# Third layer of a four-layer kernel: passage and tile order rebuilt, routing spread over the tiles, and the experts begun where the tile loop ends

## The reference

```python
proj = x @ W_in.T + b_in                      # gate, h (32 heads of 64), B, C (128 each), dt (32)
hBC = silu(conv(hBC, conv_w))                 # causal, 4 taps
dt = softplus(dt + dt_bias)
Adt = A * dt
A_cum = cumsum(A_c)                           # in chunks
Y_diag = einsum(C_c B_c * exp(segsum(A_c)), h_c)
states, carried from chunk to chunk with exp(sum of Adt)
Y_off = einsum(C_c, states) * exp(A_cum)
y = Y_diag + Y_off + D * h
g = y * silu(gate)
g = g * rsqrt(mean(g * g, -1) + EPS) * norm_w
return g @ W_out.T + b_out
```

## Time and profile before

| | |
|---|---|
| median of 3 runs | 1264.71 us (1264.55 to 1265.39) |
| profiled execution | 1266.14 us |
| its span, first to last instruction | 1264.4 us |
| busy in the span: PE, DVE, ACT, POOL | 1134.3, 899.1, 794.3, 564.4 us |
| chain that ended last, shares of the span | PE 43%, DVE 29%, ACT 15%, issue 7%, POOL 5% |

### The profile page before, as it was taken

One profiled execution on the slowest core, in us unless ns is written; L12 is line 12 of the kernel. 1 busy time (PEld: TensorE's weight loads), 2 busy tenths in 40 slices (PEclk: granted clock), 3 DMA queues, 4 the chain that ended last, 5 costly groups with the idle time before them and its releaser, 6 DMA issues.

```text
span 1264.4 us, 14530 instructions
## 1 busy us (share of the span) xinstructions
PE 1134.3 (90%) x4940; PEld 611.8 (48%) x4940; DVE 899.1 (71%) x1361; ACT 794.3 (63%) x1118; POOL 564.4 (45%) x308
## 2 busy tenths in 40 slices
PE   6788999999989999999768999999999999897887
PEld 1333344444334444444446666666666666222554
DVE  3666999999974545434589989899899998323454
ACT  4467667667542433323578888888988887435542
POOL 6002899898933846431004545545455455200000
PEclk8879999999999999999789999999999999798999
DMA  3000655555442211110021212112111111000000
GB/s 124 1 1 19 221 183 176 196 177 188 171 160 59 60 42 42 36 45 1 1 72 30 59 52 59 52 44 59 52 55 55 44 59 37 1 0 1 1 1 34
DMA packets 36807, 84.22 MB, mean 67 GB/s; under 512 B 7253, under 2 KB 13174, under 8 KB 36470
## 3 DMA queue, kind: packets, MB, share of 16 engines
q1 hardware_dynamic: 36734, 83.29, 20.9%
HBM read 80.72 MB, written 2.56 MB: 66 GB/s over the span
## 4 chain that ended last, share of the span: by engine, by line
PE 43%; DVE 29%; ACT 15%; issue 7%; POOL 5%; DMA 1%; DVEq 0%; SPq 0%; POOLq 0%; ACTq 0%
DVE work L1572 7%; DVE work L660 6%; PE ps L1010 4%; PE ps L1267 4%; PE ps L1234 4%; PE ps L1026 3%; PE ps L1018 3%; DVE yd L1633 3%; ACT work L1430 3%; ACT work L1425 3%; ACT ps L557 3%; POOL work L721 2%; DVE work L1636 2%; PE ps L441 2%; PE ps L1841 2%
## 5 line engine op out<-in xcount | busy, mean ns | idle before, releaser
L1706 POOL TENSOR_TENSOR ssum<-ssum,rs 128x1024 f32<-128x1024 f32 x32 | 75.8, 2369 | 192.9 <-DVE work L1572 190.6
L660 DVE TENSOR_TENSOR_SCAN work<-ps,work 128x1024 f32<-128x1024 f32 x64 | 146.6, 2291 | 8.3
L1572 DVE SCALAR_TENSOR_TENSOR work<-work,w_t 128x1024 f32<-128x1024 f32 x96 | 123.3, 1285 | 33.6 <-ACT work L1430 31.3
L441 PE MATMUL ps<-work,ident 128*128 128x512 f32 x256 | 121.7, 598 | 5.6 <-POOL work L721 5.4
L1000 POOL TENSOR_TENSOR work<-work,ssum 128x1024 f32<-128x1024 f32 x32 | 76.3, 2389 | 108.9 <-DVE work L1089 56.4
L557 ACT ACTIVATE ps<-work,A 128x1024 f32<-128x1024 f32 x64 | 71.6, 1118 | 72.4 <-DVE work L660 72.4
L1089 DVE TENSOR_TENSOR work<-work,ps 128x512 f32<-128x512 f32 x64 | 43.8, 687 | 99.9 <-PE ps L1018 99.8
L1068 ACT ACTIVATE work<-ps 128x512 f32<-128x512 f32 x64 | 38.1, 597 | 115.4 <-PE ps L1010 115.3
L721 POOL TENSOR_TENSOR work<-work 128x1024 f32<-128x1024 f32 x42 | 99.1, 2362 | 13.5 <-DVE work L660 13.5
L1714 POOL TENSOR_TENSOR yd<-yd,work 128x896 f32<-128x896 f32 x32 | 67.0, 2094 | 70.2 <-DVE work L1636 70.2
L1623 DVE SCALAR_TENSOR_TENSOR work<-ps,work 128x512 f32<-128x512 f32 x128 | 81.9, 682 | 0.0
(11 more groups left out here) (349 smaller groups left out, 2546.6 us busy)
## 6 DMA issues: line engine op xcount, KB each, us to landing
work<-bc_rows SPq DMA_DIRECT2D x42, 512.0 KB, 3.5
work<-sdo_rows SPq DMA_DIRECT2D x64, 224.0 KB, 3.6
yd<-bc_rows SPq DMA_DIRECT2D x22, 512.0 KB, 3.7
rs<-w_rows SPq DMA_DIRECT2D x32, 256.0 KB, 4.1
ssum<-share_rows SPq DMA_DIRECT2D x32, 256.0 KB, 3.2
w_t<-in_tile_w SPq DMA_DIRECT2D x32, 195.5 KB, 2.5
work<-in_w SPq DMA_DIRECT2D x1, 2048.0 KB, 7.9
shared<-in_f SPq DMA_DIRECT2D x3, 512.0 KB, 5.9
```

Of the source, the lines that this page charges most:

```text
L441: mm = pe.matmul(ps[:, YACC + h, :], ident[:, :], HS[u % 4][:, h * BL:(h + 1) * BL], start=(n == 0), stop=(n == DS - 1))
L660: dve.tensor_tensor_scan(h, flat_pair(DABANK), h, 0.0, ALU.mult, ALU.add).then_inc(m0["scan"], 1)
L1572: c = dve.scalar_tensor_tensor(HC[u], HP[:, tap:tap + SEQ], par(u, "taps", tap), HC[u], ALU.mult, ALU.add)
```

## The change

- Passage: B and C of the first sequence alone are prepared ahead of the loop. Step sizes and logits are one matmul of 40 columns, the logits' sigmoid is Exp on ScalarE and a sum and reciprocal on VectorE. `later`, a third triangular matrix, gives the decays in one matmul.
- The second sequence's B and C, and all routing, are done in the tiles: `beside(n)` at the head of VectorE's step, turned B in tile `B1_TURN` = 10, products in tile 11, routing in tiles 17 to 24, turned in tiles 25 and 26. In those four tiles TensorE uses `FRONT` first, and the projection of the next h comes behind the products with the states and a wait for the copy out of `FRONT`.
- Tile order: `ystar` goes ahead of the convolution; Silu of h is two halves; both halves of h are turned ahead of the first arguments.
- End: `f2_pe` starts behind the last tile's products. The last output sum and the mean squares lie between the experts; Ln and Exp are two instructions of 2048 behind the last Gelu, and VectorE scales after the last weighing.

```diff
@@ l2_sync
-                sp.wait_ge(m2["hc"], n + 1)
+                sp.wait_ge(m2["hc"], 2 * n + 2)
...
+                if n == 2:
+                    store_rows(1)
+                    store_decays(1)
@@ l2_pe, step
+                if n in (B1_TURN, B1_PRODUCT, ROUTE_TURN, ROUTE_TURN + 1):
+                    if n >= ROUTE_TURN:
+                        turn_route(n - ROUTE_TURN)
+                    else:
+                        second_sequence(n)
+                    from_states(n, b, 0)
+                    from_states(n, b, 1)
+                    if n >= ROUTE_TURN:
+                        pe.wait_ge(f2["rt_out"], n - ROUTE_TURN + 1)
+                    elif n == B1_TURN:
+                        pe.wait_ge(m2["act"], m2["bt_out1"] + 2)
+                    else:
+                        pe.wait_ge(m2["dve"], m2["gt_out1"] + 2)
                     project_h(m, b1, u1)
+                    within_chunks(n)
                     project_gate(m, b1, u1)
+                else:
...
                     turn_h(m, u1, 0)
+                    turn_h(m, u1, 1)
                     pe.wait_ge(m2["yd"], n + 1)
                     arguments(m, u1, (0, 1))
-                    turn_h(m, u1, 1)
@@ l2_act, step
+                if n == 1:
+                    decay_rows(2)
+                    decay_rows(3)
+                if n == B1_TURN:
+                    b_turned(1)
                 if more:
                     pad_h(n + 1, 1 - u)
                 if n >= 1:
                     squares(n - 1, 1 - u)
                 if more:
-                    silus(n + 1, 1 - u)
+                    silu_gate(n + 1, 1 - u)
+                    silu_h(n + 1, 1 - u)
+                    if n == B1_TURN - 1:
+                        bc_silu(1, 0)
+                        bc_silu(1, 1)
                     exponentials(n + 1)
                     weights_out(n + 1, 1 - u)
+                if n in (B1_CONV - 1, B1_CONV):
+                    bc_first_tap(1, n - B1_CONV + 1)
+                if n == ROUTE_TURN + 2:
+                    act.wait_ge(f2["rt_out"], 2)
+                    act.activation(rtb[:, :], rtf[:, :], ACT.Copy).then_inc(f2["rt_out"], 1)
@@ l2_dve
+            def beside(n):
+                if n < 2:
+                    if n == 1:
+                        dve.wait_ge(m2["dve"], m2["parts1"] + 1)
+                    three_parts(2 + n, LNDT[0:2 * H2, :, :].rearrange("p i h -> p (i h)"))
+                elif B1_CONV <= n < B1_CONV + 2 * K3:
+                    m, i = divmod(n - B1_CONV, K3)
+                    dve.wait_ge(m2["bc_tap"], 3 + m)
...
+                elif n == B1_PRODUCT:
+                    mask_products(1)
...
@@ l2_dve, step
+                beside(n)
+                dve.wait_ge((m2["sdo_in0"], m2["sdo_in1"])[u], 32 * (n // 2 + 1))
+                dve.wait_ge(m2["yoff"], 2 * n + 2)
+                dve.tensor_tensor(Y[u][:, P:], Y[u][:, P:], flat2(MID)[:, P:], ALU.mult).then_inc(m2["ystar"], 1)
                 if m < CT * BATCH:
                     convolve(m, 1 - u)
@@ f2_act
+                if n == NB * per:
+                    act.wait_ge(m2["act"], m2["rms_out"] + NB)
+                    act.preload_act_table_set("natural_log_exp_and_others")
+                    own(act.activation(flat(0, T), flat(0, T), ACT.Ln, bias=eps_t[:, :]))
+                    act.activation(flat(0, T), flat(0, T), ACT.Exp, scale=-0.5).then_inc(m2["act"], NB)
@@ f2_dve
+            scale_sums(dve, own)
             gate_dve(dve, own, f2, m2["dve"], m2["s_out"])
```

More of the change, by code:

```diff
@@ L290, in norm_act @@
             for k in range(NB):
+                if between is not None and k == NB - 1:
+                    between(0)
                 act.wait_ge(norm["centred"], NB * r + k + 1)
@@ L297, in norm_act, with top2_part @@
             root(NB - 1)
[L299 removed]
+        def top2_part(dve, own, score, ind, k, half):
             cur, eq, t, pick = rw[:, 2], rw[:, 3], rw[:, 4], rw[:, 5]
             bc = lambda m: m.unsqueeze(2).to_broadcast([P, NT, E])
[L303 to L304 removed]
+            s = score if k == 0 else cur
+            if half == 0:
                 own(dve.tensor_reduce(rm[:, 0, :], s, AX.X, ALU.max))
@@ L314, in top2 @@
                     own(dve.tensor_tensor(ind, ind, pick, ALU.add))
+        def top2(dve, own, score, ind):
+            for part in range(4):
+                top2_part(dve, own, score, ind, *divmod(part, 2))
         def split3(dve, own, w):
@@ L1294, in sum_out, with turn_route, second_sequence @@
                 mm.then_inc(m2["outp"], 1)
+            def turn_route(half):
+                pe.wait_ge(f2["dve"], f2["picked"] + 1)
+                for i in range(TB):
+                    mm = pe.transpose(ps[0:4 * E, FRONT + i // 4, (i % 4) * P:(i % 4 + 1) * P], rt[:, half * TB + i, :], ident[:, :])
+                mm.then_inc(f2["pe"], 1)
+            def second_sequence(n):
+                pe.wait_ge(m2["act"], m2["bc1"] + 2)
+                for c in range(TB):
+                    if n == B1_TURN:
+                        mm = pe.transpose(four(FRONT + c // 4)[:, c % 4, :], tile(BCH[0], TB + c), ident[:, :])
+                    else:
+                        mm = pe.matmul(four(FRONT + c // 4)[:, c % 4, :], tile(BCH[0], TB + c), tile(BCH[1], TB + c), start=True, stop=True)
+                    if c % 4 == 3:
+                        mm.then_inc(m2["pe"], 1)
             def step(n, b, t, u):
@@ new lines, in while_normed, with sums_turned @@
+            def while_normed(k):
+                if k == 0:
+                    project_bc(0, BACK)
+                if k == 1:
+                    steps_and_logits(0)
+                    steps_and_logits(1)
+                if k == 2:
+                    pe.wait_ge(m2["bc_pad"], 2)
+                    project_bc(1, BACK)
+                if k >= 2:
+                    steps_and_logits(k)
+            def sums_turned(k):
+                for i in range(8 * k, 8 * k + 8):
+                    here = slice((i % 4) * P, (i % 4 + 1) * P)
+                    pe.matmul(ps[0:H2, 4 + i // 4, here], ADT[:, i, :], upper[:, :], start=True, stop=True)
+                    pe.matmul(ps[H2:2 * H2, 4 + i // 4, here], LNDT[:, i, :], ident[:, :], start=True, stop=False)
+                    mm = pe.matmul(ps[H2:2 * H2, 4 + i // 4, here], ADT[:, i, :], fall[:, :], start=False, stop=True)
+                mm.then_inc(m2["pe"], 1)
@@ L1365, in l2_pe @@
                 mm.then_inc(m2["pe"], 1)
-            for k in range(NB):
-                if k == 2:
-                    turn_h(0, 0, 0)
-                    turn_h(0, 0, 1)
-                    pe.wait_ge(m2["act"], m2["bt_out"] + NB)
-                for i in range(4):
-                    c = 4 * k + i
-                    mm = pe.matmul(four(GT_BANK[k])[:, i, :], tile(BCH[0], c), tile(BCH[1], c), start=True, stop=True)
-                mm.then_inc(m2["pe"], 1)
-            pe.wait_ge(m2["rows_const"], 1)
+            pe.wait_ge(m2["bc_pad"], 8)
@@ L1377, in l2_pe @@
+            sums_turned(1)
+            pe.wait_ge(m2["act"], m2["cdec"] + 1)
+            for c in range(TB):
+                mm = pe.matmul(four(MID + c // 4)[:, c % 4, :], tile(BCH[0], c), tile(BCH[1], c), start=True, stop=True)
+                if c % 4 == 3:
+                    mm.then_inc(m2["pe"], 1)
+            turn_h(0, 0, 0)
+            turn_h(0, 0, 1)
+            pe.wait_ge(m2["act"], m2["bt_out"] + 2)
             arguments(0, 0, (0, 1))
```

353 lines of the change are left out of this document (185 added, 168 removed).

## The result

The changed kernel takes 1267.72 us (median of 20 runs, 1264.03 to 1272.82), the kernel before, run beside it, 1264.47 (20 runs, 1260.04 to 1266.37). The ratio is 1.0034, interval 1.0022 to 1.0046: slower by a third of a per cent, 3.3 us. The prediction was 1266.4, in a range of 1258 to 1275. The profiled execution of after took 1268.68, its span 1266.7.

What follows compares the result with a forecast made beforehand. Two loops ending together were taken to bound the tile: VectorE's with TensorE's shares, and ScalarE's. Terms -22.1 + 1.5 + 31.3 - 9.0 = +1.7 on the 1264.71 median gave 1266.4 us, range 1258 to 1275.

Steps and rivals of the forecast that it cites:

- The period: Steady loop tile with the new order: 13.24 to 13.25 us instead of 13.20, +1.5 over 30 periods.
- 8.75 + 3.45 = 12.20. So 12.24, and the convolution at 13.24: Steady tile: projection start to end of products with the states, then VectorE's decay product, then the next convolution, in us.
- a period under 13.1 or over 13.35: Sign, set in advance, that the forecast of the loop's steady tile is wrong; in us.
- Rival 2: Loop: first state does not move up, convolution at 13.44, 6 us more, so 1272; chance 0.30.
- Rival 4: Loop: earlier product shortens every tile to VectorE's 12.2, 30 x 1.0 less, so 1236; chance 0.07.
- the filler at 0.33 of idle a tile: Plain loop tiles: work added ahead of VectorE's decay product costs its length less 0.33 us idle.
- The passage: Ahead of the loop: half the preparation stays, first exponential at 633, convolution at 641.4 instead of 663.50: -22.1 us.
- What the loop takes on: Work moved into the loop's tiles (split, taps, Silus, transposes, products, routing and its turn) lengthens them: +31.3 us together.
- The end: Behind the loop: experts start before the norm, -14.4, norm's tail behind the last Gelu, +5.4: -9.0 us.
- the norm's tail: Behind the last Gelu: table load, Ln, Exp and four scalings ahead of the gate, +5.4 us.
- some 5: End: part of the experts' 14.4 us gain, ascribed to the low-clock stretch that follows the waiting.
- Rival 3: Passage: TensorE keeps its full clock, sums and products come 3 to 5 us earlier, so 1261; chance 0.20.

Runs made afterwards that it cites:

- norm_before_experts: Changed kernel with the last sum, four mean squares, Ln, Exp and scaling put back ahead of the experts: 1284.54 us, ratio 1.0151 to the changed kernel.
- product_first_alone: Kernel before with only VectorE's decay product moved ahead of the convolution (GpSimd also waits for the sum with D): 1264.83 us against 1265.11.
- product_late: Changed kernel with the decay product put back behind the convolution and the sum with D: 1256.16 us, ratio 0.9945.
- fill_all_holds: Kernel before with four unread 128x512 matmuls in TensorE's waits around the last sums and mean squares: 1261.5 us against 1264.26, ratio 0.9978.
- the kernels at 1249.55 and 1251.76: One kernel, run twice: changed kernel with the decay product behind the convolution and three ScalarE operations moved; ratios 0.9885 and 0.9917.
- late_again: Repeat run of the changed kernel with the decay product put back behind the convolution: 1252.33 us, ratio 0.9915.

## Why the prediction was nearly right, point by point

The sum was -22.1 + 1.5 + 31.3 - 9.0 = +1.7, and the traces show -24.2, +4.8, +32.4, -10.7: +2.3. The time is right to 1.3 us, but in part by luck: the terms miss by 2.1, 3.3, 1.1 and 1.7, in opposite directions. These are terms of one profile each, and the passage's can be 3 off by the clock alone, as norm_before_experts shows.

- **The period**, +1.5 predicted, +4.8 measured (0.16 x 30), and this is the step that failed. Everything up to the projection came as worked out (8.75 said, 8.70 seen). The failure is "8.75 + 3.45 = 12.20. So 12.24, and the convolution at 13.24": the stretch from the projection to VectorE's start was taken from a tile in which neither TensorE's load nor VectorE stood waiting. It is 3.65 now: 1.82 and 1.72 on TensorE, of which 0.1 is the weight load that the record before left out, and 0.11 from the end of the products' last record to VectorE. These two, less the 0.05 that the projection came earlier, put the convolution at 13.36 and not 13.24. By its own bound, "a period under 13.1 or over 13.35", this part was wrong. Rival 2 gave 13.44 by another way (a first state that does not move up); it moved up, so the rival's reason is refuted though its size was nearer (0.08 off, where the forecast was 0.12).
- **The order was no gain anywhere.** Rival 4 (VectorE's idle 1.00 is to be had) is refuted by product_first_alone, 13.36, and by product_late, 13.20. The prediction priced the order at 1.5, its cost in the period. It did price the filler at 0.33 of idle a tile (0.36 measured), but did not ask what the old order would have left: 1.0. Of product_late's 11 us, 6.7 lie there, in the taps and the routing.
- **The passage**, -22.1 and -24.2. Of the 2.1 between them 1.0 lies ahead of the passage (the layer before ends 1.0 earlier in this profile, and the norm with it); VectorE takes the step sizes at 600.77, not at 602.11, which is 0.3 more. First exponential 630.99, said 633.
- **What the loop takes on**, +31.3 and +32.4. Right within 0.4: tiles 3 to 8, 9 and 10 together, 11, 17 to 26, and the 0.5 of tile 28, which was forecast for 27. Mis-sized: tile 1 (+4.1, not +2.6) and tile 2 (+1.0, not +0.1), together 2.4. After the wait for the gate's bank, which ScalarE's padding frees, TensorE's clock is low:

```profile
651.82 1.72 PE L1259 MATMUL ps<-work 128*128 128x128 f32 x14
655.67 2.93 PE L1225 MATMUL ps<-work,w_t 128*128 128x512 f32 x4 [2.13 <-ACT work L1457]
658.53 2.65 PE L1267 MATMUL ps<-work 128*64 128x128 f32 x32
```

Four records of 512 take 2.93 where they take 1.88, and the next tile's turn is late by it. How much of the 2.4 is the clock's, norm_before_experts shows, whose loop is the same program:

```profile
658.58 1.98 PE L1225 MATMUL ps<-work,w_t 128*128 128x512 f32 x4 [2.70 <-ACT work L1457]
```

It waits longer there, 2.70, and keeps the clock; its tiles 1 and 2 are 16.87 and 13.37, together 1.6 less. So 1.6 of the 2.4 goes with the clock of this execution, and 0.8 is in both.
- **The end**, -9.0 and -10.7. Experts -16.2 where -14.4 was said, the norm's tail +5.5 where +5.4 was. The term named "some 5" as the low clock behind the waiting: fill_all_holds, in which the order is before's, has 4.8 less with the clock kept. From its 83.93 to after's 77.97 it is 6.0, which is what the order itself is worth, by one profile of each.
- **Rival 3** (full clock in the passage) came in part: the clock kept 1.00 to 604, was 0.67 from 604 to 608 and 0.90 to 612.

Left open: why product_first_alone's median equals before's, when its loop is 4.6 longer. Its profile shows the full clock at the experts as the cause of the balance; its other eleven executions have no trace. Their mean clock sorts them only loosely: 0.972 goes with the fastest (1260.22) and 0.961 with the slowest (1266.67), but those from 0.963 to 0.969 lie at 1262.5 to 1266.0 in no order.

## What to carry to other kernels

Ask of each operation whose input comes last in the period what stands behind it in its engine's queue. Here the decay product waited for TensorE's last result with the convolution behind it, and the period passed through both; put behind the convolution, it had its input long before its turn, and the filler work fitted into idle time that existed anyway (the loop went from 433.45 to 422.36 with one product moved). When a large change brings its gain and gives it back, sum the stretches between marks in both traces first: here -24, +37 and -11 under a total of +2, and the kernels at 1249.55 and 1251.76 came from work on the +37 alone. Give a short operation to the engine that is idle as its input arrives, not to the one that has always done it: ScalarE's copy of the routing made tiles 25 and 26 1.4 shorter each.

## What the runs showed of the hardware that was not expected

The lengths of TensorE's waits alone do not say whether its granted clock falls. In the end of before, waits of 2.65, 0.58 and 1.53 went with 0.70 at the last sums, 1.00 after them and 0.50 in the experts; product_first_alone, with 2.35, 1.52, 0.58 and 1.53, shows 1.00; with 0.94, 1.52, 0.58 and 1.53 it fell; with 0.94, 0.68, 0.58 and 0.67 it held. A wait of 2.69 in the passage was followed by 0.50 in norm_before_experts and by 1.00 in after, whose program is the same up to there, and behind the gate's wait in tile 1 the clock fell after 2.13 (after) and held after 2.70 (norm_before_experts, product_late, late_again). Some 5 us of an execution of these kernels go with it at the end, and 3 in the passage.

VectorE's product began 0.10 to 0.12 after TensorE's last record when it was already waiting, in every step of product_first_alone and in each plain tile of after. And a matmul's record begins with its weight load when the load itself was held by a wait, which makes the same work look 0.1 longer (697 ns against 608 for the projection's first record).
